# Splitting five u and two gate units of an input projection into rounded high and low tiles

## The reference

```python
x = x + _L0_attn_ref(_layernorm(x, axis=-1), L0_attn_W_in, ...)
# in it:
proj = hidden_states @ W_in.T               # 128 x 1024 by 1024 x 4096
u, gate = jnp.split(proj, 2, axis=-1)
x = conv_general_dilated(transpose(u), conv_w[:, None, :], ...)   # depthwise, K = 4, causal
u = silu(transpose(x) + conv_b)
ssm_p = u @ Wx.T                            # 96 columns: dt, B, C
...                                         # rms norms, delta = softplus(dt @ Wdt.T + dt_bias)
state = exp(delta * A) * state + (delta * u) * B        # scan over 64 tokens, 2048 x 16 states
y = (state . C) + u * D_param
y = y * silu(gate)
return y @ W_out.T
```

## Time and profile before

| | us |
|---|---|
| median of 3 runs | 383.94 (383.87 to 384.13) |
| the profiled execution | 383.87 |
| its span, from the first to the last instruction | 382.1 |
| TensorE busy in the span | 346.7 (91%) |
| VectorE busy | 271.5 (71%) |
| ScalarE busy | 199.0 (52%) |
| GpSimd busy | 121.3 (32%) |

### The profile page before, as it was taken

How to read it: one execution, slowest core, us unless ns; L and a number is a source line. 1 busy time by engine, 2 the same in 40 slices (tenths; PEclk the granted TensorE clock), 3 DMA queues, 4 the chain that set the end, 5 groups by cost and what they waited for, 6 DMA issues and landing times.

```text
span 382.1 us, 5181 instructions
## 1 busy us (share of the span) xinstructions
PE 346.7 (91%) x1996; PEld 223.9 (59%) x1996; DVE 271.5 (71%) x352; ACT 199.0 (52%) x397; POOL 121.3 (32%) x96
## 2 busy tenths in 40 slices
PE   0688999999899989999999979799999989899996
PEld 0335444654566656566754857588443467787785
DVE  2867067757887999998975589887820699976381
ACT  1980223179999688688702664554010379252160
POOL 2600000025999888798920020201000020210000
PEclk9999999999999999999999999999999999999999
DMA  6999999563003011166137789399999997000001
GB/s 252 421 424 407 350 422 383 208 218 112 2 1 112 0 60 51 50 211 240 50 107 237 324 333 425 120 334 332 341 420 423 409 421 307 2 3 0 0 3 55
DMA packets 12967, 81.86 MB, mean 214 GB/s; under 512 B 2109, under 2 KB 2365, under 8 KB 3661
## 3 DMA queue, kind: packets, MB, share of 16 engines
q1 hardware_dynamic: 11614, 78.23, 52.9%
q10 hardware_dynamic: 1296, 3.22, 2.5%
q0 software_dynamic: 32, 0.07, 0.0%
HBM read 80.86 MB, written 0.52 MB: 213 GB/s over the span
## 4 chain that ended last, share of the span: by engine, by line
PE 63%; DVE 15%; POOL 10%; DMA 6%; ACT 3%; issue 2%; SPq 0%; DVEq 0%; ACTq 0%; POOLq 0%
PE psum L1021 13%; PE psum L973 10%; PE psum L1141 7%; PE psum L1242 6%; DMA ring<-in_ctx 6%; PE psum L1097 5%; POOL arena L620 5%; PE psum L980 5%; PE psum L935 4%; PE psum L1165 3%; DVE rounded L1646 2%; DVE arena L1603 2%; POOL arena L623 2%; PE psum L1396 2%; PE psum L1361 2%; POOL plain L620 2%
## 5 line engine op out<-in xcount | busy, mean ns | idle before, releaser
L770 ACT ACTIVATE arena<-arena 128x126 f32<-128x126 f32 x256 | 76.5, 388 | 9.8 <-DVE arena L1603 8.8
L1021 PE MATMUL psum<-ring,hT 128*128 128x512 f32 x128 | 60.6, 602 | 0.8 <-ACT hT L686 0.8
L1603 DVE TENSOR_TENSOR_SCAN arena<-arena,psum 128x1024 f32<-128x1024 f32 x24 | 54.2, 2273 | 3.3 <-PE psum L1097 3.0
L560 POOL TENSOR_TENSOR small<-small 128x1 f32<-128x1 f32 x6 | 9.3, 1553 | 133.0 <-DVE small L1446 127.4
L620 POOL TENSOR_TENSOR arena<-arena 128x1024 f32<-128x1024 f32 x20 | 47.2, 2361 | 5.4 <-DVE arena L1603 5.4
L1646 DVE TENSOR_TENSOR rounded<-ring,rounded 128x2048 fp32r<-128x2048 f32 x16 | 36.5, 2286 | 10.2 <-ACT rounded L797 10.1
L1141 PEld LDWEIGHTS psum<-arena,ident 128*128 128x128 f32 x292 | 35.6, 192 | 13.8 <-issue 10.0
L797 ACT ACTIVATE rounded<-ring 128x2048 fp32r<-128x2048 f32 x16 | 30.6, 1912 | 24.8 <-PE psum L980 15.3
L1141 PE MATMUL psum<-arena,ident 128*128 128x128 f32 x292 | 37.3, 278 | 1.5 <-POOL arena L623 1.5
L1021 PEld LDWEIGHTS psum<-ring,hT 128*128 128x128 f32 x128 | 22.2, 190 | 27.1 <-issue 26.0
L1097 PE MATMUL psum<-plain 64*128 64x512 f32 x128 | 36.1, 641 | 1.7 <-DVE arena L1603 1.4
(11 more groups left out here) (213 smaller groups left out, 581.2 us busy)
## 6 DMA issues: line engine op xcount, KB each, us to landing
ring<-in_w_in SPq DMA_DIRECT2D x16, 1024.0 KB, 14.1
ring<-in_ctx SPq DMA_DIRECT2D x13, 1024.0 KB, 11.9
ring<-in_w_out SPq DMA_DIRECT2D x8, 1024.0 KB, 4.8
ring<-in_ctx_t SPq DMA_DIRECT2D x7, 1024.0 KB, 6.4
ring<-in_w_base SPq DMA_DIRECT2D x4, 1024.0 KB, 4.8
ring<-in_x_wk SPq DMA_DIRECT2D x4, 1024.0 KB, 7.9
ring<-in_a_wo SPq DMA_DIRECT2D x4, 1024.0 KB, 10.9
ring<-in_x_wq SPq DMA_DIRECT2D x3, 1024.0 KB, 8.9
```

The source lines that it names most:

```text
L770: last = act.activation(to, of, ACT.Exp, scale=a_par[:, k, state_no:state_no + 1])
L1021: last = pe.matmul(psum[:, proj_bank(j), :], hT[:, k, :], slot(w_in + u)[:, k % UK, :], start=(k == 0), stop=(k == KT - 1))
L1603: dve.tensor_tensor_scan(state[s % STATES], dA[:, s % 3, :], psum[:, p:p + 2, :].rearrange("p a b -> p (a b)"), 0.0, ALU.mult, ALU.add).th ...
```

## The change

Units 2, 3, 4, 6 and 7 (of u) and 8 and 9 (of the gate) are split like the later layers' units. ScalarE makes all seven high tiles, placed by hand between its other steps, VectorE makes the low tiles of the first three, GpSimd those of the other four. The high and low tile of a unit share one of three buffers, in the order 0, 1, 2, 0, 1, 2, 1; a buffer's next high tile waits for the products of the unit before it in the buffer. The left side hT is split too: high halves by ScalarE, low ones by VectorE. TensorE interleaves the three products of each k. A split unit's ring slot is free once its low tile is made. GpSimd's memset of dA's edge moves behind its low tiles.

In the diff, pool is GpSimd, act ScalarE, pe TensorE (in `w_in_product`) and dve VectorE (ahead of the first `conv_in`).

```diff
+U_SPLIT = (2, 3, 4, 6, 7, 8, 9)
+U_BUFFER = (0, 1, 2, 0, 1, 2, 1)
+U_BY_DVE = 3
...
+        u_halves = [unit_halves[n] for n in (1, 0, 2)]
...
-        for j in range(NB):
-            uses(None, (proj_psum, j + 1))
+        def u_low_signal(m):
+            return (u_low_dve, m + 1) if m < U_BY_DVE else (u_low_pool, m - U_BY_DVE + 1)
+        def u_used(u):
+            return (proj_psum, u // 2 + 1) if u % 2 else (u_even_used, sum(v <= u and v % 2 == 0 for v in U_SPLIT))
+        for u in range(2 * NB):
+            uses(u_low_signal(U_SPLIT.index(u)) if u in U_SPLIT else (proj_psum, u // 2 + 1) if u % 2 else None)
...
-            pool.memset(dA.rearrange("p s (n t) -> p (s n) t", t=L)[:, :, 0:1], 0.0).then_inc(edge_zero, 1)
...
+            for m in range(U_BY_DVE, len(U_SPLIT)):
+                pool.wait_ge(u_unit_high, m + 1)
+                unit = u_halves[U_BUFFER[m]]
+                pool.tensor_tensor(unit[:, 1, :, :], slot(first["w_in"] + U_SPLIT[m]), unit[:, 0, :, :].bitcast(F32),
+                                   ALU.subtract).then_inc(u_low_pool, 1)
+            pool.wait_ge(*u_used(8))
+            pool.memset(dA.rearrange("p s (n t) -> p (s n) t", t=L)[:, :, 0:1], 0.0).then_inc(edge_zero, 1)
...
+            act.wait_ge(hT_lo, 1)
+            act.activation(split[:, 0, 0:4, :], hT[:, 0:4, :], ACT.Copy).then_inc(u_left_high, 1)
+            act.wait_ge(hT_hi, 1)
+            act.activation(split[:, 0, 4:8, :], hT[:, 4:8, :], ACT.Copy).then_inc(u_left_high, 1)
+            def u_high(m):
+                n = first["w_in"] + U_SPLIT[m]
+                arrived(act, n)
+                if m >= U_BY_DVE:
+                    before = max(i for i in range(m) if U_BUFFER[i] == U_BUFFER[m])
+                    act.wait_ge(*u_used(U_SPLIT[before]))
+                act.activation(u_halves[U_BUFFER[m]][:, 0, :, :], slot(n), ACT.Copy).then_inc(u_unit_high, 1)
+            for m in range(U_BY_DVE):
+                u_high(m)
...
-            for j in range(3):
-                proj_copy(j)
-                last_tap(j)
-                if j:
-                    half_tanh(j - 1)
+            proj_copy(0)
+            last_tap(0)
+            u_high(3)
+            proj_copy(1)
+            u_high(4)
+            half_tanh(0)
+            last_tap(1)
+            u_high(5)
+            proj_copy(2)
+            half_tanh(1)
+            last_tap(2)
             proj_copy(3)
+            u_high(6)
             half_tanh(2)
...
+                if u in U_SPLIT:
+                    unit = u_halves[U_BUFFER[U_SPLIT.index(u)]]
+                    if k % UK == 0:
+                        pe.wait_ge(u_left_low, 2)
+                        pe.wait_ge(*u_low_signal(U_SPLIT.index(u)))
+                    pe.matmul(psum[:, proj_bank(j), :], split[:, 0, k, :], unit[:, 0, k % UK, :], start=(k == 0), stop=False)
+                    pe.matmul(psum[:, proj_bank(j), :], split[:, 0, k, :], unit[:, 1, k % UK, :], start=False, stop=False)
+                    last = pe.matmul(psum[:, proj_bank(j), :], split[:, 1, k, :], unit[:, 0, k % UK, :], start=False,
+                                     stop=(k == KT - 1))
...
+            for half in range(2):
+                v = slice(4 * half, 4 * half + 4)
+                dve.wait_ge(u_left_high, half + 1)
+                dve.tensor_tensor(split[:, 1, v, :], hT[:, v, :], split[:, 0, v, :].bitcast(F32),
+                                  ALU.subtract).then_inc(u_left_low, 1)
+            for m in range(U_BY_DVE):
+                dve.wait_ge(u_unit_high, m + 1)
+                unit = u_halves[U_BUFFER[m]]
+                dve.tensor_tensor(unit[:, 1, :, :], slot(first["w_in"] + U_SPLIT[m]), unit[:, 0, :, :].bitcast(F32),
+                                  ALU.subtract).then_inc(u_low_dve, 1)
```

More of the change, by code:

```diff
@@ L300, in perceiver @@
         q_done = sem("q_done")
+        u_left_high = sem("u_left_high")
+        u_left_low = sem("u_left_low")
+        u_unit_high = sem("u_unit_high")
+        u_low_dve = sem("u_low_dve")
+        u_low_pool = sem("u_low_pool")
+        u_even_used = sem("u_even_used")
         edge_zero = sem("edge_zero")
-        conv_halved = sem("conv_halved")
         first_tap = sem("first_tap")
@@ L760, in decay @@
                 if s == 0:
-                    act.wait_ge(edge_zero, 1)
+                    act.wait_ge(edge_zero, 2)
                 if s >= 3:
@@ L1016, in w_in_product @@
                     pe.wait_ge(*((proj_sb, j - 2) if j <= NG else (proj_sb, j) if j > NG + 1 else (projT_read, NG)))
+                at = dict(start=(k == 0), stop=(k == KT - 1))
+                if u in U_SPLIT:
[7 more added lines that the diff above has]
+                                     stop=(k == KT - 1))
+                    if k % UK == UK - 1:
+                        last.then_inc(proj_psum if k == KT - 1 else u_even_used, 1)
+                    return
                 if k % UK == 0:
@@ L1020, in w_in_product @@
                     arrived(pe, w_in + u)
-                last = pe.matmul(psum[:, proj_bank(j), :], hT[:, k, :], slot(w_in + u)[:, k % UK, :], start=(k == 0),
-                                 stop=(k == KT - 1))
+                last = pe.matmul(psum[:, proj_bank(j), :], hT[:, k, :], slot(w_in + u)[:, k % UK, :], **at)
                 if k % UK == UK - 1:
@@ L1503, in _ @@
             variance(1)
+            dve.wait_ge(hT_hi, 1)
+            for half in range(2):
[8 more added lines that the diff above has]
+                                  ALU.subtract).then_inc(u_low_dve, 1)
             dve.wait_ge(mamba_in, 80)
-            dve.wait_ge(edge_zero, 2)
+            dve.wait_ge(edge_zero, 1)
             def conv_in(g):
@@ L1542, in silu @@
                                          op1=ALU.mult).then_inc(gated, 1)
-            dve.tensor_scalar(small[:, 320:416], small[:, 320:416], 0.5, None, ALU.mult).then_inc(conv_halved, 1)
-            dve.wait_ge(conv_halved, 1)
+            step(dve.tensor_scalar(small[:, 320:416], small[:, 320:416], 0.5, None, ALU.mult))
             conv_in(0)
```

## The result

The changed kernel takes 403.19 us (median of 4 runs, 400.75 to 403.29) beside 384.01 us of the kernel before (4 runs, 383.87 to 384.13): ratio 1.0484, 95% interval 1.0457 to 1.0511, so 4.8% slower. The forecast was 404.0. The profiled execution has a span of 401.3 us (before: 382.1).

A forecast was written before the change was run, and what follows sets the result against it. TensorE was taken as the bound until about 66 us. Its savings vanish in waits; the late first copy and four 4.54 us hold-ups, walked through the ring, delay the first scan by 20.3: 383.9 + 20.3 = 404, range 389 to 407.

The forecast's parts named there:

- What the change saves: TensorE in the input projection: 0.70 us per split unit, 4.9 us for seven, 3.5 of them by unit 7.
- the ring: Each 512-channel group's loop: projection copy, four transposes, conv-in on VectorE, last tap on ScalarE, other taps on VectorE, tanh, silu.
- Step A: ScalarE, ahead of the first projection copy: unit 4's high tile waits for its transfer; copy at 48.8 us, not 43.13 (+5.7).
- Step B: Convs on VectorE: each GpSimd low tile falling into a conv holds up the taps for its full 4.54 us.
- The sum: Delays walked through the convs: last silu starts at 94.2 us instead of 73.55, first scan +20.3, 404 us in all.
- TensorE's pace: TensorE after its gaps: a possible fall to 1.2 GHz, nothing in the sum, up to 3 us if taps aren't held up.
- What would show it: Trace signs: first copy about 48.8 us, single taps about 4.8, last silu 94, first scan 108, TensorE waits some 25.
- Not held up: Rival: GpSimd doesn't hold up the taps, only the late first copy stays; 389 us, up to 392; chance 0.18.
- Partly held: Rival: one of four low tiles falls beside tanh and tap, or GpSimd's take 3.8 us; 392 to 399; chance 0.12.
- Faster: Rival: TensorE's chain decides and the side engines keep up; 4.9 us less, 379 us; chance 0.04.

The follow-up runs named there:

- e7: The changed kernel with only units 2 and 3 split, both low tiles on VectorE, ScalarE's order as before the change: 382.62 us, ratio 0.9965 to the kernel before.
- e4: The changed kernel with unit 4's high tile behind the first copy and last tap, its low tile behind conv 0: 399.27 us, ratio 1.0392.
- e1: The changed kernel with GpSimd's four low tiles cut to eight columns, all else kept: 387.63 us, ratio 1.0089.
- e5: The changed kernel with unit 4's tiles behind the first group's steps and GpSimd's low tiles cut to eight columns: 387.53 us, ratio 1.0095.
- e9: The kernel of e5 with 18 idle products filling TensorE's wait ahead of unit 4: 385.73 us, ratio 1.0045.
- e2: The kernel before with four added GpSimd subtractions of 128x2048 on data that nothing reads: 400.27 us, ratio 1.0431.
- e3: The kernel before with four added GpSimd operations that only write (iota of 128x4096), in the places of e2's subtractions: 384.01 us, ratio 0.9997.
- e8: The changed kernel with idle products filling TensorE's two long waits before the transposes of groups 0 and 2: 403.15 us, ratio 1.0499.
- e6: The changed kernel with all seven low tiles on VectorE, the four later ones between its steps: 392.51 us, ratio 1.0223.

## Why the prediction was right

**What the change saves**: 0.70 us a unit is confirmed by e7 (1.39 us for two). That all of it vanishes in the waits is what the changed kernel shows: the first scan is late by the ring's delay, with nothing given back.

**Step A** was right in place and size: copy at 48.73 (said 48.8), with the wait for DMA in front of its high tile, conv 0 begun at 53.79. What it costs by itself no run shows. e4, which undoes it, is 3.9 us faster, but 3.3 of these are hold-ups that fell elsewhere. Conv 0 begins 5.96 us late and the hold-ups are 17.1 us, 23.0 in all, and the first scan is late by 19.2: 3.8 us went into idle time that VectorE had in the ring before. With the hold-ups gone, undoing it brings nothing at first (e1 to e5), because the low tile moved with it makes TensorE wait and fall to 1.2 GHz; with that wait filled (e9) the kernel is 1.9 us below e1.

**Step B** was right: four hold-ups, two in conv 0 and one each in convs 1 and 2. The GpSimd subtraction took 4.52 to 4.71 us (said 4.54, out of two smaller shapes). They cost the taps 8.48 us in conv 0 and 4.29 and 4.31 in convs 1 and 2, 17.1 together where four times 4.54 would be 18.2. That is the term that was too large: a held tap's row starts a little behind the subtraction's and ends a little behind its end (55.76 against 55.58 us and 60.43 against 60.29 for the first), its own 0.35 us included. The place where the rows of the scan stage had left a doubt, fused operations, is settled by e2 and e3. The Trainium skill ("SBUF — State Buffer", section "SBUF: two separate sides") makes the condition a GpSimd operation that reads SBUF; e3 agrees with it, with 3.49 us of taps beside 10.84 us of iotas.

**The sum** came out 0.8 us high (404.0 against 403.19), and 1.05 at the first scan; its last step, 383.9 + 20.3, is 404.2 and was rounded down. Its steps, said and measured: conv 0 ends at 66.4 and 65.8, conv 1 at 76.8 and 75.9, conv 2 at 87.3 and 86.1, the last silu starts at 94.2 and 92.8, the first scan at 108.4 and 107.35. The error grows by 0.6, 0.2 and 0.3 us over convs 0 to 2, 1.2 us, of which the hold-ups are 1.1. From the last silu to the scan I had taken 14.2 us (20.65 us of delay became 20.3 without a reason); it was 14.6, as before.

**TensorE's pace**: the prediction left open whether the fall to 1.2 GHz comes, and said that it would cost nothing here. It came (0.69 from 50 to 54 us, 0.50 from 70.5 to 76), and e8 gives 403.15 with the two long waits filled. The products at 15.84 us that it was read from took 0.63 us each in a stretch in which the granted clock of the profile is 1.00, which the prediction didn't say; the changed kernel's trace shows the fall in the clock itself. e5 and e9 show the limit of that: 1.8 us as soon as TensorE sets the ring.

**What would show it** named 25 us of waits for TensorE; they were 17.3 (44 to 94 us). An estimate from the granted clock of the stretches between 50 and 90 us in which it was busy throughout gives some 5.9 us by which the products took longer at half pace and filled such waits; the rest of the difference is open.

**The rivals.** Not held up (389): e1 is that case, 387.63, and the changed kernel isn't. Partly held (392 to 399): all four subtractions fell into a conv and none took less than 4.52 us; e4 is near that case, with one beside the silu. Faster (379), the reading of the chain of waits that TensorE's time is what there is to gain: true of two units (e7); with all seven and nothing held up it still took 385.73 us (e9), and no number between was tried.

Not shown: who gets the next turn. That a waiting subtraction gets in between two taps, and one tap between two subtractions, is what the timelines of the changed kernel and of e2 fit; no run varied it. Nor was it tried whether GpSimd would do no harm if the taps read one operand from PSUM; that the conv-in of e4 is not held speaks for it.

## What to carry over

Before handing an idle engine work, look at what it shares with the busy one: a GpSimd subtraction of two SBUF tensors takes VectorE's two-input operations out for nearly its whole length (4.2 to 4.3 us of some 4.6 here), about twice what the same subtraction takes on VectorE (2.28 us), so "idle" was not free. In a ring of short steps over several engines a copy placed by hand ahead of a step delays the step by what its own input is late, so try it behind the step, and see what then waits for its other half. When an engine's clock falls in waits, ask who waits for that engine: TensorE's fall to 1.2 GHz cost nothing in the changed kernel and 1.8 us in e5.

## What the runs showed of the hardware that was not expected

A queued transfer's landing is not the same in each execution. Unit 4, issued at 23.8 to 24.0 us in each of the eleven profiled executions, took between 20.5 us (e1) and 23.6 us (e6) to land; the changed kernel had 23.0, with nothing different from e1 ahead of it:

```profile
44.36 1.91 ACT L722 ACTIVATE arena_halves<-ring 128x2048 fp32r<-128x2048 f32 x1 [4.20 <-DMA ring<-in_w_in]
```

44.36 against 46.92 is 2.56 us. This execution is e1's fastest, 385.28 us where the median is 387.63. That the landing makes the spread of times is likely for e1 but not shown, for only one execution of each kernel was recorded, and it is no rule: e8 waits for the same transfer and stays within 0.2 us, while e2 and e4, whose first copy doesn't wait for it, vary by 1.4 and 2.1 us. Part of the spread goes with TensorE's pace: in e1 and e5 the slower executions also have the lower mean granted clock (e1 388.98 us at 0.990, 387.63 at 0.996; e5 388.27 at 0.991, 387.19 at 0.996).
